# Cross-attention block: keys' three bf16 parts stored once, batch 0 prepared first, key scores and exponential taken head by head

## What is computed

```python
def _L0_xattn_ref(Q, K, V, mask, Wq, bq, Wk, bk, Wv, bv, Wo, bo):   # Q: layernorm of x, K = V = ctx_1024 (4, 2048, 128)
    q = (Q @ Wq.T + bq).reshape(B, Sq, 16, 8).transpose(0, 2, 1, 3)
    k = (K @ Wk.T + bk).reshape(B, Sk, 16, 8).transpose(0, 2, 1, 3)
    v = (V @ Wv.T + bv).reshape(B, Sk, 16, 8).transpose(0, 2, 1, 3)
    scores = einsum('bhqd,bhkd->bhqk', q, k) / sqrt(8) + mask
    out = einsum('bhqk,bhkd->bhqd', softmax(scores), v)
    return out.transpose(0, 2, 1, 3).reshape(B, Sq, 128) @ Wo.T + bo
x = x + xattn(layernorm(x), ctx, ctx, mask, ...)
x = x + attn(layernorm(x), W_in, W_out, Wp, ...)   # weights divided by max(largest singular value, 1); scan over 128 steps
x = x + ffn(layernorm(x), w1, b1, w2, b2)          # binarised weights, exact gelu
```

## Time and profile before

| what | us |
|---|---|
| median of 3 runs | 326.34 |
| profiled execution: time | 329.18 |
| profiled execution: span | 327.4 |
| PE busy in the span | 257.0 |
| VectorE busy | 231.3 |
| ScalarE busy | 200.7 |
| GpSimd busy | 108.2 |
| chain that ended last, share of PE | 58% |
| mean granted clock of TensorE | 0.895 |

### The profile page before, as it was taken

How to read it: one execution, slowest core, us unless ns; L and a number is a source line. 1 busy time by engine, 2 the same in 40 slices (tenths; PEclk the granted TensorE clock), 3 DMA queues, 4 the chain that set the end, 5 groups by cost and what they waited for, 6 DMA issues and landing times.

```text
span 327.4 us, 9590 instructions
## 1 busy us (share of the span) xinstructions
PE 257.0 (79%) x3904; PEld 160.6 (49%) x3904; DVE 231.3 (71%) x425; ACT 200.7 (61%) x309; POOL 108.2 (33%) x267
## 2 busy tenths in 40 slices
PE   0799615499999999999999999999999877550276
PEld 0577401245555556555565655555655444440156
DVE  4358839267878788787878989879888940538941
ACT  1267700267777777877777777777876665195042
POOL 7123421115434553345433665232113120104210
PEclk9999955569999999999999999999999996785559
DMA  6926979941535415344263312311321000000001
GB/s 146 381 88 220 226 179 292 363 153 50 148 92 153 146 50 161 107 127 145 52 188 102 103 50 77 73 50 50 80 68 52 3 4 2 0 0 0 0 0 32
DMA packets 24565, 34.48 MB, mean 105 GB/s; under 512 B 2444, under 2 KB 19112, under 8 KB 24392
## 3 DMA queue, kind: packets, MB, share of 16 engines
q1 hardware_dynamic: 23716, 33.37, 35.0%
q0 software_dynamic: 128, 0.14, 0.5%
q10 hardware_dynamic: 676, 0.33, 0.3%
HBM read 20.20 MB, written 13.63 MB: 103 GB/s over the span
## 4 chain that ended last, share of the span: by engine, by line
PE 58%; ACT 17%; SPq 6%; DMA 6%; DVE 6%; issue 5%; POOL 2%; POOLq 0%; ACTq 0%; DVEq 0%
PE ps L447 15%; ACT probs L739 13%; PE ps L434 13%; PE ps L418 6%; PE ps L320 4%; PE ps L357 4%; SPq L259 4%; PE ps L487 3%; PE ps L495 3%; DMA k_rows_dram<-k_parts 2%; DMA w_kv<-in_L_xattn_Wq_dram 2%; PE ps L455 2%; PE ps L667 2%; PE ps L340 2%; DMA ctx_buf<-in_ctx_dram 1%
## 5 line engine op out<-in xcount | busy, mean ns | idle before, releaser
L1191 DVE TENSOR_REDUCE pmax<-ps 128x2 f32<-128x1024 f32 x128 | 156.1, 1224 | 42.8 <-PE ps L418 41.0
L739 ACT ACTIVATE probs<-ps 128x1024 f32<-128x1024 f32 x128 | 130.8, 1022 | 47.2 <-PE ps L434 47.2
L447 PE MATMUL ps<-probs,v_now 128*9 128x128 f32 x2048 | 82.4, 280 | 0.2 <-ACT probs L739 0.2
L434 PE MATMUL ps<-q_max,k_rows 51*128 51x128 bf16 x1024 | 52.3, 223 | 13.9 <-ACT probs L739 12.8
L447 PEld LDWEIGHTS ps<-probs,v_now 128*9 128x9 f32 x2048 | 43.8, 91 | 34.9 <-issue 33.1
L418 PE MATMUL ps<-k_rows,q_now 48*128 48x512 bf16 x256 | 51.2, 398 | 11.0 <-DMA k_rows<-k_rows_dram 8.3
L968 POOL CAST max_cols<-negmax 128x2 bf16<-128x2 f32 x32 | 6.1, 192 | 133.6 <-DVE negmax L1197 133.6
L434 PEld LDWEIGHTS ps<-q_max,k_rows 51*128 51x128 bf16 x1024 | 30.0, 96 | 37.5 <-ACT probs L739 22.7
L418 PEld LDWEIGHTS ps<-k_rows,q_now 48*128 48x128 bf16 x256 | 12.8, 96 | 14.2 <-DMA k_rows<-k_rows_dram 8.5
L690 ACT ACTIVATE ctxT<-ps 128x512 f32<-128x512 f32 x16 | 9.6, 597 | 14.2 <-PE ps L320 14.2
L357 PE MATMUL ps<-power 128*128 128x128 f32 x96 | 16.7, 297 | 0.2 <-DVE power L1119 0.2
(11 more groups left out here) (184 smaller groups left out, 360.0 us busy)
## 6 DMA issues: line engine op xcount, KB each, us to landing
k_rows<-k_rows_dram SPq DMA_DIRECT2D x64, 192.0 KB, 3.3
k_rows_dram<-k_parts SPq DMA_DIRECT2D x16, 384.0 KB, 3.8
ctx_buf<-in_ctx_dram SPq DMA_DIRECT2D x16, 256.0 KB, 5.5
k_rows_dram<-k_parts SPq DMA_DIRECT2D x16, 256.0 KB, 3.7
k_rows_dram<-k_parts SPq DMA_DIRECT2D x16, 128.0 KB, 4.1
mask_sb<-in_mask_1x1xSxS_ff_dram SPq DMA_DIRECT2D x1, 1024.0 KB, 9.3
q_all<-q_rows_dram SPq DMA_DIRECT2D x2, 384.0 KB, 6.5
w_nat<-in_L_ffn_w_dram SPq DMA_DIRECT2D x2, 256.0 KB, 8.8
```

The source lines that it names most:

```text
L434: t = pe.matmul(dst, k_rows[rows, i % 4, at:at + P], q_max[rows, i % 2, :], start=not masked, stop=True, skip_group_check=masked)
L447: t = pe.matmul(ps[at:at + HEAD_COLS, 6, 0:P], v_now[:, i % 2, 4 * c + j, HEAD_COLS * h:HEAD_COLS * h + HEAD_COLS], probs[:, c, h, P * j:P ...
L739: act.activation(probs[:, u % CHUNKS, :, :], ps[:, 4:6, :], ACT.Exp).then_inc(probs_ready, 1)
L1191: dve.tensor_reduce(pmax[:, i % 2, :, c], ps[:, bank:bank + 2, :], AX.X, ALU.max).then_inc(pmax_ready, 1)
```

## The change

- The keys' three parts are stored once per chunk (384 KB, one DMA instead of three of 768 KB together). A load of one head is two DMAs: 48 rows read through a source pattern that repeats the 24 rows (8 channels by 3 parts) twice, and 8 rows of part 0. The operand has 56 rows instead of 48; query rows are laid out to match, three times part 0, three times part 1, once part 2.
- Order of the start: context 0 and the key weight first; chunks 0 to 3 and the queries of batch 0 alone are prepared ahead of the loop's first scores; pair 0 is loaded in four quarters of keys, the odd head's later halves and pairs 1 to 3 from GpSimd's queue. Chunks 4 to 7 and the other queries are projected between the first eight units' scores, and GpSimd splits chunks 4 to 7 after the maximum's split of pairs 0 to 3, chunks 8 to 15 from pair 4 on.
- SP: stores of chunks 4 and 5, the other queries' stores, contexts 8 and 9, weights, query load, vectors, contexts 10 and 11, stores of chunks 6 and 7, then pair 4 and the rest. The context buffer has 6 slots instead of 8.
- Loop: key scores of head 0 of g+1, scores of g+8, key scores of head 1, value product; the exponential is two instructions of 512 columns. `q_now` and `v_now` with their copies are gone; operands are read in place.
- All 24 squarings are in the loop, four in eight units from unit 64, normalised every fourth; the Gram products are at unit 55, the first norm sum at unit 63. The mask's check is a sum of magnitudes on ScalarE.

```diff
-SQ_PERIOD = 3
-TINY = 1e-30
+SQ_PERIOD = 4
+TINY = 1e-36
...
-    K_GROUPS = ((0, 3), (3, 2), (5, 1))
-    BLOCKS = 6
...
+    TRIPLE = HD * PARTS
+    ROWS = 2 * TRIPLE + HD
     ALL_ROWS = ROWS + PARTS
     HALF_ROWS = 64
-    LOADS = 32
+    LOADS = 16 * 4
 
...
+        def store_k(eng, n):
+            b, c = divmod(n, CHUNKS)
+            eng.dma_start(k_dram[b, :, :, 512 * c:512 * c + 512], k_parts[:, :, 512 * n:512 * n + 512]
+                          ).then_inc(k_stored[b % 2] if b else k_first[c], 16)
+
+        def load_half_pair(eng, i, h, keys, loaded):
+            b, p = divmod(i, PAIRS)
+            at, first = HALF_ROWS * h, 16 * p + HD * h
+            n = keys.stop - keys.start
+            triples = k_dram[b, first:first + HD, :, keys].rearrange("r i n -> (r i) n")
+            eng.dma_start(k_rows[at:at + 2 * TRIPLE, i % 4, keys],
+                          triples.rearrange("(a m) n -> a m n", a=1).broadcast_to((2, TRIPLE, n))).then_inc(loaded, 16)
+            eng.dma_start(k_rows[at + 2 * TRIPLE:at + ROWS, i % 4, keys], k_dram[b, first:first + HD, 0, keys]
+                          ).then_inc(loaded, 16)
+
...
+        first_tokens, rest_tokens = slice(0, T), slice(T, TOK)
...
             load_ctx(0)
-            sp.dma_start(w_kv[:, 1, :], Wv).then_inc(ld["kv"], 16)
...
+            sp.dma_start(w_kv[:, 0, :], Wk).then_inc(ld["wk"], 16)
+            for n in range(1, EARLY):
+                load_ctx(n)
+            sp.dma_start(w_kv[:, 1, :], Wv).then_inc(ld["wv"], 16)
+            sp.dma_start(mask_sb[:, :], mask.rearrange("a b q k -> (a b q) k")).then_inc(ld["mask"], 16)
+            for n in range(EARLY, CTX_SLOTS):
+                load_ctx(n)
+
...
+            def store_chunk(n):
+                sp.wait_ge(k3_ready, n + 1)
+                store_k(sp, n)
+
...
+            store_q_parts(first_tokens, 0, 1)
+            store_chunk(0)
+            sp.wait_ge(once("q_stored"), 16 * 3)
+            sp.wait_ge(once("q_all_zeroed"), 1)
+            load_q(sp, first_tokens, once("q_loaded"))
+            sp.wait_ge(once("k_ones_ready"), 1)
+            store_chunk(1)
+            for c in range(2):
+                sp.wait_ge(k_first[c], 16)
+                for h in range(2):
+                    load_half_pair(sp, 0, h, slice(512 * c, 512 * c + 512), k_first[c])
+                load_ctx(CTX_SLOTS + c)
+                store_chunk(2 + c)
+            for c in (2, 3):
+                sp.wait_ge(k_first[c], 16)
+                load_half_pair(sp, 0, 0, slice(512 * c, 512 * c + 512), k_first[c])
+            for i in range(1, 4):
+                load_half_pair(sp, i, 0, all_keys, k_rows_loaded[i])
+            for n in range(EARLY, EARLY + 2):
+                store_chunk(n)
+            store_q_parts(rest_tokens, 4, 2)
+            load_ctx(FIRST)
+            load_ctx(FIRST + 1)
+            sp.dma_start(w1_nat[:, :, :], w1.rearrange("(a p) d -> p a d", p=P)).then_inc(ld["mlp"], 16)
+            sp.dma_start(w2_nat[:, :], w2).then_inc(ld["mlp"], 16)
             sp.dma_start(w_nat[:, W_IN, :], W_in).then_inc(ld["ssm"], 16)
             sp.dma_start(w_nat[:, W_OUT, :], W_out).then_inc(ld["ssm"], 16)
-            for n in range(2, FIRST):
+            sp.wait_ge(once("q_stored"), 16 * 6)
+            load_q(sp, rest_tokens, once("q_loaded"))
+            for v, at in ((bv, BV), (alpha_log, ALPHA), (delta_bias, DBIAS), (bp, BP0), (b1, B1_0)):
+                n = v.shape[0] // P
+                sp.dma_start(vec_nat[at:at + n, :], v.rearrange("(a p) -> a p", p=P)).then_inc(ld["vec"], 16)
+            sp.dma_start(w_nat[:, W_O, :], Wo).then_inc(ld["w"], 16)
...
-            for h in range(2):
-                sp.dma_start(q_all[HALF_ROWS * h:HALF_ROWS * h + ROWS, :, :, :].rearrange("r p b t -> r p (b t)"),
-                             q_dram.rearrange("(p h r) i n -> h (r i) p n", p=PAIRS, h=2)[h]
-                             ).then_inc(once("q_loaded"), 16)
-            store_k(3)
-            sp.wait_ge(once("k_ones_ready"), 1)
-            sp.wait_ge(k_stored_first, 16 * len(K_GROUPS) * CHUNKS)
-            for i in range(4):
-                load_pair(i)
-            for n in range(CHUNKS, FIRST):
-                store_k(n)
-            small_vectors()
-            for n in range(FIRST, ALL_CHUNKS):
-                load_ctx(n)
...
+            for n in range(EARLY + 2, FIRST):
+                store_chunk(n)
             for i in range(4, ALL_PAIRS):
                 if i % PAIRS == 0:
-                    sp.wait_ge(k_stored_rest, 16 * len(K_GROUPS) * CHUNKS * (i // PAIRS))
+                    sp.wait_ge(k_stored[i // PAIRS % 2], 16 * CHUNKS * (2 if i // PAIRS == 3 else 1))
                 load_pair(i)
+                if i % 2 == 1 and FIRST + 4 + (i - 5) // 2 < ALL_CHUNKS:
+                    load_ctx(FIRST + 4 + (i - 5) // 2)
                 if i >= 6 and i % 2 == 0 and FIRST + i // 2 - 3 < ALL_CHUNKS:
-                    store_k(FIRST + i // 2 - 3)
+                    store_chunk(FIRST + i // 2 - 3)
 
...
-            def keyscores(u, masked):
+            def keyscores(u, h, masked):
                 i, c = divmod(u, CHUNKS)
-                if c == 0:
+                if c == 0 and h == 0:
                     pe.wait_ge(q_max_ready, i + 1)
-                wait(pe, probs_ready, u)
+                wait(pe, probs_ready, 2 * u - 1 + h)
+                rows = slice(HALF_ROWS * h, HALF_ROWS * h + ALL_ROWS)
                 for j in range(4):
-                    for h in range(2):
-                        rows = slice(HALF_ROWS * h, HALF_ROWS * h + ALL_ROWS)
-                        dst = ps[:, 4 + h, P * j:P * j + P]
-                        if masked:
-                            mask_key(dst, c, j, j == 0)
-                        at = 512 * c + P * j
-                        t = pe.matmul(dst, k_rows[rows, i % 4, at:at + P], q_max[rows, i % 2, :],
-                                      start=not masked, stop=True, skip_group_check=masked)
+                    dst = ps[:, 4 + h, P * j:P * j + P]
+                    if masked:
+                        mask_key(dst, c, j, j == 0)
+                    at = 512 * c + P * j
+                    t = pe.matmul(dst, k_rows[rows, i % 4, at:at + P], q_max[rows, i % 2, :],
+                                  start=not masked, stop=True, skip_group_check=masked)
                 t.then_inc(keyscores_ready, 1)
...
             def attend(masked):
-                for u in range(6):
...
+                scores(0, masked)
+                early_k(4)
+                early_turn(5)
+                early_v(4)
+                scores(1, masked)
+                early_k(5)
+                early_turn(6)
+                pe.wait_ge(v_ready, 3)
+                pe.wait_ge(once("xn_ready"), B)
+                turn_xn(6, 1, B - 1)
+                early_v(5)
+                scores(2, masked)
+                early_k(6)
+                early_turn(7)
+                pe.wait_ge(once("qT_ready"), 4)
+                pe.matmul(ps[:, 6, T:TOK], kvT[:, 2, :], xnT[:, T:TOK], start=True, stop=True
+                          ).then_inc(once("q_done"), 1)
+                early_v(6)
+                scores(3, masked)
+                early_k(7)
+                scores(4, masked)
+                early_v(7)
+                scores(5, masked)
                 pe.wait_ge(once("out_bank_zeroed"), 1)
                 turn_max(0).then_inc(turned, 1)
-                for u in range(6, LEAD):
-                    scores(u, masked)
-                keyscores(0, masked)
+                pe.wait_ge(ctxT_ready, FIRST)
+                pe.wait_ge(k32_ready, FIRST - EARLY)
+                scores(6, masked)
+                keyscores(0, 0, masked)
+                keyscores(0, 1, masked)
+                scores(7, masked)
+                pe.wait_ge(v_ready, FIRST)
...
                 for g in range(UNITS):
                     i = g // CHUNKS
                     if g + 1 < UNITS:
-                        keyscores(g + 1, masked)
+                        keyscores(g + 1, 0, masked)
                     if g + LEAD < UNITS:
                         scores(g + LEAD, masked)
+                    if g + 1 < UNITS:
+                        keyscores(g + 1, 1, masked)
                     pv(g)
                     if g == 0:
                         pe.wait_ge(q_max_ready, 1)
...
             def exp_unit(u):
-                act.wait_ge(keyscores_ready, u + 1)
                 wait(act, pv_done, u - 3)
-                act.activation(probs[:, u % CHUNKS, :, :], ps[:, 4:6, :], ACT.Exp).then_inc(probs_ready, 1)
+                for h in range(2):
+                    act.wait_ge(keyscores_ready, 2 * u + h + 1)
+                    act.activation(probs[:, u % CHUNKS, h, :], ps[:, 4 + h, :], ACT.Exp).then_inc(probs_ready, 1)
...
+            rest_root()
+            gp.wait_ge(once("k_ones_ready"), 1)
+            for c in range(CHUNKS):
```

(49 more changed lines are left out.)

649 lines of the change are left out of this document (316 added, 333 removed).

## The result

The changed kernel takes 459.06 us (median of 4 runs, 456.63 to 462.46), the kernel before on the same chip 326.67 (326.28 to 327.78): 1.405 times as long, with a 95% interval of 1.394 to 1.416. The forecast was 346, its range ended at 358. Of the rivals, B (the loads get slow) has the sign and the mechanism, and even its 423 is short by 36.

A forecast was written before the change was run, and what follows sets the result against it. TensorE was taken to bound the unit loop. Start -1, units 8 to 15 +1, eight octets (eight units each) +16, squarings +2 and +6, end -4: +20 on 326.3 gives 346 us, range 322 to 358.

The forecast's parts named there:

- B: Key loads: a leading count of 2 puts each on 2 of 16 engines, 9.0 us a pair; about 423 us, chance 0.17.
- 3.3 us to landing: Key loads: time from issue to landing, assumed for pair 4 and for octets (eight units) with a chunk to split.
- the queue wait of "0.9 per octet": SP's queue: waiting for GpSimd's chunk before an odd pair's load adds 0.9 us to each of eight eight-unit octets.
- the second long gap of the start: Start, before unit 16's scores: TensorE's second long idle time brings the clock to 0.50, some 2 us of loss.
- Key scores head by head, +0.2 us per unit: Unit loop: four key-score passes per head stand alone on TensorE, adding 0.2 us per unit, +1.1 per eight units.
- rival C: Unit loop: passes of different row groups overlap, so the head split costs TensorE nothing; 322 us, chance 0.21.
- The end's -4: Last units: exponential in halves shortens the period from 1.52 to about 1.1 us, giving back 4 us in all.
- The squarings, +1.5 per octet together with the heads: Squaring stage: more squarings in the loop and the head split raise eight units from 13.3 to 14.8 us.
- The first exponential at 36: Start: first exponential at about 36 us, between 31 and 41, 21 us earlier than before.
- The context's wait and pair 4's: SP's queue: chunk 8's context delays side work to 49.5 us, pair 4's load puts unit 16's scores at 76.5.
- The early start as a whole: Start through unit 16: a gain of about 0 to 1 us, with bounds of -5 to +5.
- rival D: Whole kernel: early start and longer units cancel exactly, 328 to 326 us; chance 0.06.

The follow-up runs named there:

- e1: Kernel before with each key load's source being 24 rows repeated by a leading dimension of 2, (2, 24, 2048); 395.9 us, ratio 1.217.
- e2: Kernel before with the 24 source rows leading and the repeat of 2 inside, (24, 2, 2048); 327.69 us, ratio 1.009.
- e10: Kernel before with each key load's source being 12 rows repeated by a leading dimension of 4, (4, 12, 2048); 336.34 us, ratio 1.031.
- e4_inter: Changed kernel with the two copies of each head's 24 rows interleaved, leading count 24, query rows stored to match; 389.86 us, ratio 1.199.
- e6_inter_steady: e4_inter with only the stores of chunks 8 to 15 moved behind the odd pairs' loads; 339.79 us, ratio 1.037.
- e3_heads: Kernel before with only key scores and exponential head by head, the later unit's scores between the heads; 323.7 us, ratio 0.9955.
- e9_pair4: e4_inter with SP's contexts 8 and 9 earlier, later stores behind loads, pair 4's load directly behind chunk 5's store; 312.71 us, ratio 0.961.

## Why the prediction was wrong, point by point

**The step that failed first: 3.3 us to landing**, taken for the new load from the old one's median. No row showed a large transfer that leads with 2, I took the likelier value to be the known one, and left the other end out of the range as rival B at 0.17. The measured landing is 10.2 us behind the last issue for unit 16 and 9.4 to 9.8 in the late stage; e1, e2 and e10 show the cause with nothing but the source pattern changed: two engines, and not all 16, carry the load. The Trainium skill (DMA: Bandwidth & Descriptors, "Why a DMA increments its semaphore by 16 and not by 1") gives the number of engines as the largest, up to 16, that divides the leading sizes of both patterns. The runs agree: shares of 0.13 with 2 in front and 0.25 with 4, and 0.77 with 24 in front of 48 rows written, where the rule gives twelve. The same page ("Rules for kernel authors") names a leading zero-step copy as a case that confines a transfer, which the changed kernel's 57 GB/s at a share of 0.16 bears out. I had written that by it B would be the forecast, and gave it a sixth. Rival B's own arithmetic, 22 GB/s an engine and 9.0 us a pair, was right to 5% (8.5 measured); its 423 fell short by 36. Of these, 15 are the eight octets from unit 32 to 95 (24.3 us each, where B had 22.4, by the second error below) and 9 the way to unit 16 (15.8 us late, where B had 7); the other 12 are not assigned.

**The second: the queue wait of "0.9 per octet".** The wait was named with its chain and its place. Its length in e4_inter is 2.3 us instead of 0.9: the chain takes 11.1 us and not 10, with half of the difference in the issues (2.1 us for the three ahead of the landing, where I had 1.6 for four) and a quarter in the scores and the maximum (1.9 against 1.65), and the load is due after 8.4 us and not 9.0 (137.2 to 145.6, where the key scores of the next unit stand alone). The larger miss is that I priced only the idle time. I counted a loss by the clock for the second long gap of the start, some 2 us, and none for the short gaps of the loop. But 2.3 us of idle time in front of an octet that has no other slack put the clock to 0.50 for 10 us, 5 us lost, and the slower units then delay the next maximum, which is the start of the same chain. Eight octets at about 20.4 us instead of 14 are the 50 us that e6_inter_steady gets back. In the changed kernel, with both causes, units 32 to 95 take 194.4 us.

**Key scores head by head, +0.2 us per unit:** wrong, measured 0.06, covered by the exponential's waits that went (rival C's mechanism). The order of starts in the rows before was the evidence I used against it; there each group had both heads alternating, so it could not tell program order from order within each head. The end's -4 was nearly right: e3_heads is 0.7 us ahead of the kernel before at the scores of unit 96 and 3.7 at the last exponential.

**The squarings, +1.5 per octet together with the heads:** the six octets of squarings, from the scores of unit 72 to those of unit 120, take 79.1 us before, 78.2 in e3_heads (three squarings an octet, head by head) and 80.6 in e9_pair4 (four). So both together cost 0.25 an octet and not 1.5. The step from e3_heads to e9_pair4 is 0.4 an octet for the fourth squaring and all else that differs between the two, where I had 0.65 for the squaring.

**The first exponential at 36:** it came at 45.2. First scores at 25.5 were 3.5 late. From there to the scores of unit 7 (45.9) it took 20.5 us, where I allowed 15. The key and value projections of chunks 4 to 7 fill most of this stretch, but they are not the excess: e4_inter has the same projections, its unit 7 stands at 41.0, 15.5 us after the first scores, and its first exponential at 40.3, inside my 31 to 41. The 4.9 us between the two kernels are the form of the load again. In the changed kernel TensorE stands still in front of unit 2, whose keys are in the third quarter, where e4_inter does not, and the granted clock behind it is 0.62 and 0.52 (36 to 38, 38 to 40 us):

```profile
36.02 0.39 PE L453 MATMUL ps<-k_rows,q_all 56*128 56x512 bf16 x2 [2.76 <-issue]
```

**The context's wait and pair 4's:** both came, for the reasons given. The context of chunk 8 was turned at 62.39 after an idle time of 12.9 us (forecast 49.5 and 10), unit 16's scores at 94.7 (76.5). The early start as a whole, "worth about 0 to 1 us", did not hold either: with SP's order as it was it loses even when the loads are quick (unit 16 at 83.4 in e4_inter, 78.9 before), since each of the two waits is about 12 us (11.7 and 11.6). With the queue cleared it gains: e9_pair4 reaches unit 16 18.7 us ahead of the kernel before and keeps 14.7 of that to the last exponential.

**The range** left out B. With a row that was missing and a rule that named this very pattern, 358 as the upper end was not the bound that the unknown cost called for. Two smaller slips: rival C's sum gives 321 and not 322, and rival D's 346 - 10 - 7 is 329.

## What to carry to other kernels

Read a DMA's access pattern from the outside in: the first dimension that is not 1, repeats included, limits how many of the 16 engines share the work (here 2 gave two, 4 gave four, 24 gave about twelve). Put a repeat inside and lay the rows out to match. In a queue that issues in program order, a store that waits for a late producer belongs behind every load that is due before that producer can be done. And price an idle time of a TensorE-bound loop with the clock after it: here 2.3 us of waiting cost about 7.

## What the runs showed of the hardware that was not expected

- Leading counts of 2, 4 and 24 for the same 192 KB: 395.9, 336.3 and 327.7 us, or 1.217, 1.031 and 1.009 of the kernel before, and DMA shares of 0.13, 0.25 and 0.77 inside a load. With 2, a pair needs 8.5 us.
- Passes on the lower and the upper 64 rows of the array do not keep one common order: a pass of the scores on the upper rows started 50 ns ahead of two passes of key scores on the lower rows that precede it in the program. The order of starts that the prediction held against rival C is not what these records show.
- After a gap of 2.3 us the granted clock stayed at 0.50 for 10 us although TensorE was busy without a break.
- Issued by GpSimd, loads with a leading count of 2 still landed only after a median of 4.5 us, but the two of a pair ran side by side (DMA share 0.26), where SP's had a share of 0.13 and together took 8.5 us.
- An SP issue of a load with the repeat inside takes 0.77 us, with the repeat in front 0.59 to 0.65, of the plain 8 rows 0.46; the old load's median is 0.42.
